# Layer 1 cross attention: TensorE makes the value rows of a step in front of its scores instead of behind them

## The reference

```
q, k, v = (_split_heads(x @ w.T + b) for the queries, the context as keys, the context as values)
scores = jnp.einsum('bhqd,bhkd->bhqk', q, k) / jnp.sqrt(HEAD_DIM)
mask = causal[None, None] | (k_idx >= valid_len)
scores = jnp.where(mask, neg, scores)
attn = jax.nn.softmax(scores, axis=-1)
out = jnp.einsum('bhqk,bhkd->bhqd', attn, v)
return out @ w_o.T + b_o
```

## Time and profile before

| | |
|---|---|
| median of 3 runs | 2389.85 us (2385.58 to 2390.87) |
| profiled execution | 2388.07 us |
| its span, first to last instruction | 2386.3 us |
| busy in the span | PE 1818.3 (76%), DVE 1732.9 (73%), ACT 1101.2 (46%), POOL 748.7 (31%) |
| steps of the stage | L640 from 755.9 us to 1008.3 us, granted clock 1.00 in every step shown |

### The profile page before, as it was taken

One profiled execution on the slowest core, in us unless ns is written; L12 is line 12 of the kernel. 1 busy time (PEld: TensorE's weight loads), 2 busy tenths in 40 slices (PEclk: granted clock), 3 DMA queues, 4 the chain that ended last, 5 costly groups with the idle time before them and its releaser, 6 DMA issues. The chain is left out here.

```text
span 2386.3 us, 36354 instructions
## 1 busy us (share of the span) xinstructions
PE 1818.3 (76%) x11979; PEld 1108.3 (46%) x11991; DVE 1732.9 (73%) x5474; ACT 1101.2 (46%) x3070; POOL 748.7 (31%) x649
## 2 busy tenths in 40 slices
PE   6997989962887999989998775665555555556888
PEld 3545547542355777744465452333333333333453
DVE  4446342268765666657647689999999999997665
ACT  3653442251314777721233755555555555555411
POOL 0300045005434555410034403454333333431230
PEclk8999999965999999999999995666566666667979
DMA  5000101310000000000200000000000000000000
GB/s 223 2 1 1 44 14 30 105 68 1 2 2 1 2 2 2 2 1 0 99 2 1 2 1 1 1 1 1 1 1 1 1 1 0 1 1 1 1 1 18
DMA packets 10597, 37.89 MB, mean 16 GB/s; under 512 B 1344, under 2 KB 7488, under 8 KB 9136
## 3 DMA queue, kind: packets, MB, share of 16 engines
q1 hardware_dynamic: 8880, 33.05, 3.6%
q0 software_dynamic: 1536, 2.59, 0.4%
HBM read 30.17 MB, written 5.51 MB: 15 GB/s over the span
## 5 line engine op out<-in xcount | busy, mean ns | idle before, releaser
L3726 PE MATMUL psum<-work 32*128 32x256 f32 x512 | 131.0, 657 | 291.9 <-ACT work L3844 291.9
L3906 DVE MATCH_REPLACE8 work<-work 128x256 f32<-128x256 f32 x768 | 305.8, 411 | 0.0
L3969 POOL TENSOR_TENSOR work<-work 128x1024 f32<-128x1024 f32 x63 | 148.2, 2352 | 484.0 <-ACT work L3844 477.8
L3903 DVE MAX8 work<-work 128x8 f32<-128x256 f32 x768 | 267.0, 411 | 0.0
L3726 PEld LDWEIGHTS psum<-work 32*128 32x128 f32 x512 | 78.3, 313 | 318.3 <-ACT work L3844 162.8
L842 POOL TENSOR_TENSOR work<-work 128x256 f32<-128x256 f32 (+1 forms) x128 | 103.0, 826 | 127.3 <-DVE work L791 123.6
L3844 ACT ACTIVATE work<-work 128x256 f32<-128x256 f32 x256 | 128.4, 502 | 0.0
L3751 PE MATMUL psum<-work,tiles 128*8 128x256 f32 x512 | 116.2, 606 | 8.2 <-ACT work L3854 7.4
L3971 POOL TENSOR_TENSOR work<-work 128x1024 f32<-128x1024 f32 x63 | 119.2, 1892 | 6.1 <-DVE work L3928 1.2
L3842 ACT ACTIVATE work<-psum,work 128x256 f32<-128x256 f32 x256 | 117.4, 459 | 0.0
L739 ACT ACTIVATE work<-work 128x128 f32<-128x128 f32 (+1 forms) x256 | 112.8, 451 | 0.0
(11 more groups left out here) (644 smaller groups left out, 4636.7 us busy)
## 6 DMA issues: line engine op xcount, KB each, us to landing
big_weights<-L0f_dram SPq DMA_DIRECT2D x1, 6103.5 KB, 28.2
big_weights<-L_dram SPq DMA_DIRECT2D x1, 5772.0 KB, 16.7
big_weights<-L_dram SPq DMA_DIRECT2D x1, 4952.5 KB, 16.8
choice_rows<-tiles SPq DMA_DIRECT2D x2, 1024.0 KB, 10.4
tiles<-choice_rows SPq DMA_DIRECT2D x8, 256.0 KB, 5.1
big_weights<-L_dram SPq DMA_DIRECT2D x1, 2027.0 KB, 21.2
big_weights<-L_dram SPq DMA_DIRECT2D x1, 1644.5 KB, 13.6
big_weights<-L0f_dram SPq DMA_DIRECT2D x1, 1644.5 KB, 6.4
```

The source lines that it names most:

```text
L3726: mm = nc.tensor.matmul(scores(n)[:, u, :], qb[head, tile % 2, u % 2 * P:(u % 2 + 1) * P], kb[head, tile % 2, :], start=True, stop=True, t ...
L3903: ch.step(v.max(top8[:, n % 2, u, r, :], src[:, u, :]))
L3906: ins = v.match_replace(raw[:, n % 2, u, :], top8[:, n % 2, u, r, :], src[:, u, :], REPLACED)
L3969: ch.link(g.tensor_tensor(mine, mine, rest[:, n % 2], ALU.subtract))
```

## The change

In the loop, `make_values(s)` stands in front of `score(s)`. The wait for `v_taken` (VectorE has read out the values of the step before, L786, and with them all that lies in the banks) goes from `score` to `make_values`, since that is now the first to write the banks. The wait for ScalarE's queries stays with `score`. Nothing else is changed; the lists of VectorE, ScalarE, GpSimd and SyncE are the same. In the changed file the scores have line 638.

```
@@ -632,8 +632,6 @@
             def score(p):
                 pe.wait_ge(c.qk_taken.sem, c.qk_taken.at(4 * p + 4))
-                if p >= 1:
-                    pe.wait_ge(c.v_taken.sem, c.v_taken.at(p))
                 for x in range(2):
...
             def make_values(p):
                 if p % PER == 0:
                     pe.wait_ge(c.staged.sem, c.staged.at(p // PER + 1))
+                if p >= 1:
+                    pe.wait_ge(c.v_taken.sem, c.v_taken.at(p))
                 for x in range(2):
@@ -695,8 +695,8 @@
                 if s < PAIRS:
+                    make_values(s)
                     score(s)
-                    make_values(s)
                 if s + 1 < PAIRS:
                     keys(s + 1)
```

## The result

| | before | changed |
|---|---|---|
| median of 9 runs each | 2388.02 us (2384.96 to 2392.43) | 2397.73 us (2394.66 to 2399.72) |
| ratio, 95% interval | | 1.0037 (1.0027 to 1.0047), 8.9 us |
| span of the profiled execution | 2386.3 us | 2395.9 us |
| busy PE / DVE / ACT / POOL | 1818.3 / 1732.9 / 1101.2 / 748.7 | 1830.0 / 1728.2 / 1102.2 / 749.1 |
| the stage: first L619 to the first product (L284) of the next | 270.86 us | 272.70 us |

Slower by over 0.2%, which the prediction gave a chance of 0.15, and outside its range. The profile of the changed kernel, read in the order of the prediction, shows the stage as it was worked out.

The account below looks back on a forecast made before the run. The prediction took TensorE to bound the stage, with about 0.19 us per change of tile shape. Its terms, 4.31 − 1.37 − 0.90 − 0.19 = +1.9 us on a median of 2389.85, gave 2391.7 us, range 2387.0 to 2396.0.

Parts of the forecast that it names:

- What bounds the stage: TensorE bounds the stage: busy for all 8.02 us of an ordinary step and 8.15 of a long step's 8.45.
- the price of a tile change: One more change of tile shape on TensorE per step, +0.196 us each, +4.31 us over 22 ordinary steps.
- The row from another stage: L3260 and L3242, whole array to row tiles and back: 0.10 + 0.29 = 0.39 us for two changes.
- The rival in which the fourth change is free: Ordinary steps stay at 8.02 us and long ones fall to that: sum −3.8 us, 2386.1; chance 0.07.
- VectorE earlier: VectorE's L771 starts 2.10 us after the step's start instead of 2.32; everything up to L781 comes 0.21 earlier.
- the six long steps: VectorE's L781 comes ahead of GpSimd's mask operation L3061; steps take 8.22 instead of 8.45 us, −1.37 us in all.
- The rival in which GpSimd keeps its port between two operations: L3061 goes before L781, long steps stay 8.45: +3.2 us, 2393.1; chance 0.29 together with VectorE no earlier.
- the slower rival: L781 also loses to GpSimd's L3057 and is held for all of it: +5.9 us, 2395.8; chance 0.10.
- Start and end: Start of the stage: ScalarE's table load and L662 0.90 us earlier, −0.90; end, step 31: L781 earlier, −0.19 us.
- The stage's sum: Tile changes, long steps, start and end together: 4.31 − 1.37 − 0.90 − 0.19 = +1.9 us.
- The median: Whole kernel's time: 2391.7 us forecast, from a median of 2389.85 before; chance 0.81 of staying within 0.2%.
- the stage's cases: +1.9 us (0.50), +3.2 to +3.4 (0.29), +5.9 (0.10), −3.8 (0.07), the rest 0.04.

Follow-up runs that it names:

- before_again: The kernel before, unchanged, measured against itself; ratio 0.9998 (0.9989 to 1.0007).

## Why the prediction was wrong

**What bounds the stage, and the price of a tile change.** Right. (The forecasts of this part add up to +1.85, which the prediction rounds to +1.9.) Ordinary steps were to grow by 0.196 and grew by 0.195 (8.220 against 8.024 to 8.025), in all four executions of the changed kernel. The excess over the pace of the columns is now 0.21 for L650, 0.21 for the scores and 0.11 for L619. The row from another stage carried this: no row of the stage itself had the pair of shapes. The rival in which the fourth change is free is out.

**VectorE earlier, the six long steps.** Right. In step 14 L771 came 2.06 after the start of the step (2.10 forecast), L781 took 0.22 (0.18), the steps 8.22. The rival in which GpSimd keeps its port between two operations is out: L781 won against L3061 in all six, and it lost in step 2, where it came second, as forecast. The L781 beside an L3057 took 0.22 as well, so the slower rival had no ground either. The Trainium skill ("SBUF — State Buffer", Who interferes with whom) says that the order of issue decides who is blocked. The traces agree: 0.22 us where L781 came first (step 14), 1.09 where it came second (step 2).

**Start and end.** Right: −0.90 for the table load and L662, and L797 of step 31 came 3.62 after the step's start instead of 3.82.

**The stage's sum**: +1.85 forecast, +1.83 to +1.84 in the four traces of the changed kernel.

**The median.** Here it failed. The prediction said of the total that "each case spreads by some 2 us", and built its range of 2387.0 to 2396.0 as the stage's cases plus that; the median came at 2397.73. The step took the 2115 us outside of the stage as a constant, because the edit leaves them alone, and took the spread from three runs. The page before had a hint: a granted clock below 0.8 of full speed in 16 of its 40 slices. But 13 of the 16 lie in the stretch from 1411 us on that takes the same time in every trace; what moved was the stretch ahead of the stage from 468 to 743 us (266.6 to 278.9 in the fourteen traces, at 0.80 in the trace before) and the shorter ones behind, where TensorE is busy for most of the time and loses what a half clock costs. What the runs showed in its place: one kernel's profiled executions differ by up to 19 us outside of the stage, and medians of 5 to 12 runs of one kernel against before by 11 us. With such a term the range should have been some ±8 us around the same centre (an estimate from these differences), and the chances of faster and slower far nearer to each other. The mechanism of the stage was right; the term that failed is the one for the rest of the kernel.

Is the changed kernel slower, then? By 1.84 us in its stage, shown in four traces. Of the total, three comparisons with 11 or 12 runs each (0.9997, 0.9999, 0.9999) say level, and one says 8.9 us slower. The nine runs of the result all lie above all nine of the kernel before, which a plain scatter of single runs doesn't give, nor would a shift that loses its clock everywhere. The two kernels moved apart from both sides: the kernel before had a median of 2388.0 there and of 2391.8 to 2394.0 in the four later sets, the changed one 2397.7 there and 2390.3 to 2391.2 later. **What stays open** is what makes whole sets of runs lie high or low: the chip, the order of the runs, or something at the start of a set. No run here separates them, and I don't claim that the shift has no part in it on some chip.

## What to carry to other kernels

Price a move on TensorE by the shapes of its neighbours, not only by its own instructions: groups on the whole array, on row tiles and on column tiles cost 0.19 to 0.20 us at each boundary here on average, and an order with one boundary more pays that in every step. Where a small VectorE operation falls together with one of GpSimd's that holds it up, look at who arrives first; 0.2 us earlier turned 1.02 into 0.22. And read an edit of a few us from the length of its own stage in the traces, several of them: here that gave 1.84 four times over, while the ratio of the totals gave anything from −0.03% to +0.37% for the same kernel.

## What the runs showed of the hardware

The granted clock also falls inside the tail of the stage in some executions and not in others, with the same instructions. The last 17 us of the stage in before_again, and the last 14 in before:

```profile
1008.00:1025.19 17.19, 12.06 (x81) 8.57 (x79) 7.30 (x31) 7.61 (x28) 5.60 (x7) 0.90 0.00 1
```

```profile
1010.00:1024.00 14.00, 8.88 (x67) 6.18 (x66) 6.54 (x27) 6.65 (x23) 3.95 (x5) 1.00 0.01 1
```

There TensorE waits in turn for VectorE (1.20 us), GpSimd (1.58 and 0.88) and ScalarE (0.68), the same in both traces to 0.01 us, and has worked without a pause in the steps until then. In before_again the last L662 group takes 1.54 us instead of 0.88 and the L673 behind it 1.91 instead of 1.03. With the fall the stage took 272.41, without it 270.86: 1.55 us, nearly the price of the whole change. The length of this stage therefore comes in two values for one kernel, and two traces can be compared only when both have the fall or neither has.

The second surprise is the size of the gap in which a port is won: L781 arrives 0.16 before L3061 in step 14 and goes first although an L842 is still running and L3061 follows that without a gap; in step 2 it is 0.03 late and waits for all of L3061's 1.09 us.
